# A Mamba-like mixer and a Hadamard FFN on one core: order of the prologue and of the FFN's residual work

## The chip, the cores and the metric

One core of a Trainium2 chip runs the whole kernel in one launch. The metric is the device time in microseconds (us), the median of three runs. Engines: PE (TensorE), DVE (VectorE), ACT (ScalarE), POOL (GpSimd), and SP (SyncE), which only issues DMAs here.

## The reference

The input `u` has 4 batches of 512 tokens by 256 channels. `c` (4 x 256) gives six vectors per batch, shift, scale and gate for each of two halves:

```
sa, ca, ga, sb, cb, gb = silu(c) @ wmod          (ga, gb: sign(g) * max(|g|, 0.25))
h = layernorm(u) * (1 + ca) + sa
xBC, z, A = split(h @ W_in.T)                    32 heads, head 8 wide, state 64
x, B, C = split(causal_conv4(xBC) + conv_b)
M[l, s] = (C_l . B_s) * exp(segsum(-softplus(A)))  for s <= l, per head
y = M x + D x ;  u1 = u + ga * (y * silu(z + z_bias)) @ W_out.T
h2 = layernorm(u1) * (1 + cb) + sb
out = u1 + gb * fwht(silu(h2 @ W1.T) * (h2 @ W3.T)) @ W2.T     hidden 1024
```

All of it is float32.

## The kernel before, in words

Every engine has one instruction stream, written out by hand, with semaphores between them; the order in the text is the order on the engine. A matrix product that needs float32 is made of three matmuls with high and low parts (`split_mm`, L334 to L336).

The **prologue** works by batch b of u. DVE makes the statistics (L938 to L944) and, with the inverse root from POOL (L1260), the normalised rows `xn` (L951). PE transposes them with the identity out of `cst` into banks 2 and 3 (L356). ACT applies shift and scale (`h32`, L700) and copies a high part (L704), POOL subtracts the low part (L1266). PE then projects: the decay inputs from `h32` (`a_project`, L387), two channel tiles of x from the high and low parts (`x_project`). ACT does the convolution's last tap of each tile with its bias (L711), DVE the other three (L974). The tiles of x go to DRAM by SP, and through PE transposes (L402) and an ACT copy (L718) into `x_tok`. The decays go through softplus (ACT L732 to L737, DVE L1009), a running sum (DVE L1013), DRAM, and back as rows broadcast over the partitions. In between PE makes the modulation vectors (`modulation`, L345) and the gate rows (L366), which go over DRAM into `gates`. While it waits for data PE does `warm` matmuls on zeros (L425).

The **loop** has 8 groups of 4 heads by 4 batches, 32 units. For each unit PE projects four tiles of B and C (`proj`), ACT and DVE do the taps (L751, L1054), PE makes scores (L499), ACT the decays (L789), DVE `mix` (L1042), PE the states (L518), the inter and intra parts (L534, L543). A unit's stages stand in three successive steps. POOL masks the sums rows (L1317) and splits weights. Before the loop proper the units of group 0 are written out: unit (0,0) with the prologue, then step(0,1), (0,2), (0,3).

The **tail** is the FFN by batch: `up` (8 hidden tiles m: two products of 512 columns, silu on ACT, `hid` L1183 and `hid_lo` L1190 on DVE) and `down` (L334 to L336 with 256 columns). The front of the next batch is put in between the hidden tiles: the sum of y at m = 0, the gate (L1082) at m = 2, the output projection (PE L603) at m = 4, two residuals of two instructions each (L1145, L1149) at m = 6, the statistics at m = 7.

Of the kernel before, what the change touches and what calls it, by code (L numbers as in the profile page):

```python
# [46 lines left out]
def adaln_ssm_ffn_kernel(nc, u, w_bc, w_x, w_a, w_z, conv, d_rows, z_bias, w_out, w13, w2, c_t, wmod,  # L47
                         consts, out, sums_d, gates_d):
    with ExitStack() as ctx:
# [279 lines left out]
        def _(pe):  # L329
# [40 lines left out]
            def x_project(b):  # L370

                pe.wait_ge(s["hlo_done"], KT * (b + 1))
                for xt in range(2):
                    if b >= 2:
                        pe.wait_ge(s[f"xtaps{xt}"], 3 * (b - 1))
                    for kt in range(KT):
                        i = split_mm(ps[:, GT * (b % 2) + xt, :], wx_hi[:, xt, kt, :], wx_lo[:, xt, kt, :],
                                     ht_hi[:, kt, b * L:(b + 1) * L], ht_lo[:, kt, b * L:(b + 1) * L],
                                     kt == 0, kt == KT - 1)
                    i.then_inc(s["xp_mm"], 1)  # L380
# [11 lines left out]
            def x_transposes(b):  # L392

                for xt in range(2):
                    n = 2 * b + xt
                    pe.wait_ge(s[f"xtaps{xt}"], 3 * (b + 1))
                    if n >= 2:
                        pe.wait_ge(s["xtok_ev"], n - 1)
                    else:
                        pe.wait_ge(s["h32_done"], KT * B)  # L400
                    for c in range(CH):
                        i = nc.tensor.transpose(ps[:, 2 + xt, c * P:(c + 1) * P],  # L402
                                                acc[:, n // GT, n % GT, c * P:(c + 1) * P], ident)
                    i.then_inc(s["xT_mm"], 1)
# [1076 lines left out]
```

## Time and profile before

| | |
|---|---|
| three timed runs | 585.65, 585.75, 586.25 us (median 585.75) |
| the profiled execution | 584.53 us, span 582.7 us, mean granted clock 0.994 |
| busy share of the span | PE 97%, DVE 81%, ACT 66%, POOL 35% |
| DMA | 70.93 MB, mean 122 GB/s |

How to read it: "start, us" are microseconds from the span's start; "idle before <-" is the engine's idle time ahead of an instruction and what ended it. PE's ends are modelled, since matmuls overlap, so its start times are the firmer numbers. PEclk is the clock that was granted to PE as a share of full speed.

### The profile page before, as it was taken

Reading aid. Unit: us, or ns where it says so; the run is one execution under the profiler, and the core shown is the slowest. Engines: PE = TensorE matmul, PEld = TensorE weight load, DVE = VectorE, ACT = ScalarE, POOL = GpSimd, SP = SyncE. Lnnn points to the kernel's source line nnn. Section 1 sums busy time; section 2 is a strip of 40 time slices with the busy share of each in tenths; the row PEclk is TensorE's granted clock in tenths of the full one; section 3 lists DMA queues with packets and bytes.
Section 4 is the critical chain, followed back from the end, with each engine's and each line's share of the span. In section 5 each row is a group of like instructions: output and inputs, shape, how many; then the busy total and the mean of one; then the engine's idle time right before and its main releaser. Section 6 shows DMA issues by size and latency. Waiting matters only on the chain.

```text
span 582.7 us, 18096 instructions
## 1 busy us (share of the span) xinstructions
PE 563.0 (97%) x6693; PEld 452.1 (78%) x6694; DVE 472.7 (81%) x753; ACT 386.8 (66%) x960; POOL 206.2 (35%) x377
## 2 busy tenths in 40 slices
PE   7899999999999999999999999999998998998997
PEld 3577677778778787777777877877687987988987
DVE  6789999989989989988999999999657637637443
ACT  2588788788888888877878888887633223332340
POOL 4742265464464365686245243445000000000000
PEclk9799999999999999999999999999999999999999
DMA  8535544533534535533443447456423034100101
GB/s 288 231 115 191 152 142 121 163 116 114 163 106 126 162 108 194 165 109 108 132 147 112 126 151 192 149 162 176 133 74 108 1 97 120 37 2 0 37 0 37
DMA packets 39516, 70.93 MB, mean 122 GB/s; under 512 B 4532, under 2 KB 10804, under 8 KB 39224
## 3 DMA queue, kind: packets, MB, share of 16 engines
q1 hardware_dynamic: 39480, 70.47, 38.6%
q8 instruction: 20, 0.33, 0.2%
q14 instruction: 16, 0.13, 0.1%
HBM read 57.34 MB, written 13.12 MB: 121 GB/s over the span
## 4 chain that ended last, share of the span: by engine, by line
PE 81%; DVE 9%; ACT 3%; issue 3%; DMA 2%; POOL 1%; SPq 0%; DVEq 0%; ACTq 0%; POOLq 0%
PE ps L334 17%; PE ps L336 16%; PE ps L335 16%; PE ps L499 10%; PE ps L543 5%; PE ps L482 4%; PE ps L534 4%; PE ps L518 4%; PE ps L603 2%; DVE acc L1054 2%; DMA u_sb<-in_u 1%; DVE mix L1042 1%; DVE hid_lo L1190 1%; PE ps L356 1%; PE ps L387 1%
## 5 line engine op out<-in xcount | busy, mean ns | idle before, releaser
L1054 DVE SCALAR_TENSOR_TENSOR acc<-ps,cw_dve,acc 128x511 f32<-128x511 f32 (+2 forms) x384 | 259.1, 739 | 2.9 <-ACT acc L751 1.4
L789 ACT ACTIVATE decay<-sums,p_slot 128x128 f32<-128x128 f32 x512 | 160.6, 396 | 1.3 <-DVE mix L1042 0.5
L1317 POOL TENSOR_SCALAR_AFFINE_SELECT sums<-sums 128x512 f32<-128x512 f32 x128 | 81.6, 640 | 180.6 <-DMA sums<-running_sums 172.7
L751 ACT ACTIVATE acc<-ps,cw_act 128x512 f32<-128x512 f32 x128 | 93.2, 776 | 48.9 <-PE ps L543 45.4
L334 PE MATMUL ps<-ht_hi,wg_hi 128*128 128x512 f32 x256 | 106.9, 418 | 2.0 <-POOL wg_lo L1255 1.1
L336 PE MATMUL ps<-ht_hi,wg_lo 128*128 128x512 f32 x256 | 101.1, 395 | 0.0
L335 PE MATMUL ps<-ht_lo,wg_hi 128*128 128x512 f32 x256 | 101.0, 395 | 0.0
L1042 DVE TENSOR_TENSOR mix<-ps,decay 128x1024 f32<-128x1024 f32 x64 | 78.0, 1219 | 20.6 <-PE ps L499 19.3
L499 PE MATMUL ps<-acc 64*64 64x64 f32 (+1 forms) x2048 | 69.8, 255 | 0.7 <-DVE mix L1042 0.7
L889 ACT ACTIVATE silu_sb<-ps 128x512 f32<-128x512 f32 x32 | 19.2, 599 | 77.3 <-PE ps L336 77.3
L499 PEld LDWEIGHTS ps<-acc 64*64 64x64 f32 x2048 | 54.4, 132 | 9.7 <-issue 9.0
L334 PEld LDWEIGHTS ps<-ht_hi,wg_hi 128*128 128x128 f32 x256 | 48.1, 188 | 14.7 <-issue 1.5
L1183 DVE TENSOR_TENSOR hid<-ps,silu_sb 128x512 f32<-128x512 f32 x32 | 22.1, 691 | 45.5 <-ACT silu_sb L889 45.5
L336 PEld LDWEIGHTS ps<-ht_hi,wg_lo 128*128 128x128 f32 x256 | 48.0, 187 | 11.7
L1260 POOL TENSOR_TENSOR rstd<-vareps,minus_half 128x4 f32<-128x4 f32 x8 | 8.2, 1027 | 135.4 <-DVE vareps L944 131.7
L335 PEld LDWEIGHTS ps<-ht_lo,wg_hi 128*128 128x128 f32 x256 | 48.2, 188 | 7.7
L334 PE MATMUL ps<-h_hi,w_hi 128*128 128x512 f32 x128 | 50.7, 396 | 0.8 <-DVE h_lo L1164 0.8
L336 PE MATMUL ps<-h_hi,w_lo 128*128 128x512 f32 x128 | 49.9, 390 | 0.0
L335 PE MATMUL ps<-h_lo,w_hi 128*128 128x512 f32 x128 | 49.9, 389 | 0.0
L334 PE MATMUL ps<-w_hi,hid_hi 128*128 128x256 f32 x128 | 36.9, 288 | 5.0 <-DVE hid_lo L1190 4.8
L335 PE MATMUL ps<-w_lo,hid_hi 128*128 128x256 f32 x128 | 36.2, 283 | 0.0
L336 PE MATMUL ps<-w_hi,hid_lo 128*128 128x256 f32 x128 | 36.2, 282 | 0.0
(136 smaller groups left out, 897.4 us busy)
## 6 DMA issues: line engine op xcount, KB each, us to landing
sums<-running_sums SPq DMA_DIRECT2D x128, 256.0 KB, 3.3
y_parts<-yt_sb SPq DMA_DIRECT2D x32, 256.0 KB, 2.0
wg_raw<-in_w_bc SPq DMA_DIRECT2D x8, 512.0 KB, 4.6
stage<-y_parts SPq DMA_DIRECT2D x16, 256.0 KB, 4.2
u_sb<-in_u SPq DMA_DIRECT2D x4, 512.0 KB, 7.1
stage<-in_w SPq DMA_DIRECT2D x1, 2048.0 KB, 15.3
x_channels<-acc SPq DMA_DIRECT2D x8, 256.0 KB, 2.3
ee<-decay_rows SPq DMA_DIRECT2D x8, 256.0 KB, 4.4
```

Source lines behind the costliest of these rows:

```text
L334: mm(o, w_hi, x_hi, start=first, stop=False)
L335: mm(o, w_hi, x_lo, start=False, stop=False)
L336: return mm(o, w_lo, x_hi, start=False, stop=last)
L482: i = nc.tensor.transpose(ps[:, 6, c * P:(c + 1) * P], acc[:, b % 2, p, c * P:(c + 1) * P], ident)
L499: i = mm(ps[NS * h:NS * (h + 1), 2 + a, c * P + NS * h:(c + 1) * P], acc[own, b % 2, p, c * P + NS * h:c * P + NS * (h + 1)], acc[own, b % ...
L518: i = mm(o, b_tok[:, p, c * P + NS * a:c * P + NS * (a + 1)], xds[:, b % 2, V0[c]:V0[c] + n, HD * j:HD * (j + 1)], start=(c == 0), stop=(c ...
L543: i = mm(ps[QD * j:QD * j + YW, 7, c * P:(c + 1) * P], xs[:, b % 2, c, j, :], mix[:, j, c * P:(c + 1) * P], start=False, stop=True, skip_g ...
L751: af(acc[:, b % 2, t, :], ps[:, PROJ_BANK[t], :], ACT.Identity, bias=cw_act[:, t, 1:2], scale=cw_act[:, t, 0:1]).then_inc(s[f"tap_a{t}"], 1)
L789: i = af(decay[:, j, c * P:(c + 1) * P], sums[:, j, c * P:(c + 1) * P], ACT.Exp, scale=-1.0, bias=p_slot[:, b * CH + c, j:j + 1])
L1042: tt(mix[:, 2 * p:2 * p + 2, :], ps[:, 2:4, :], decay[:, 2 * p:2 * p + 2, :], ALU.mult).then_inc(s["mixed"], 1)
L1054: stt(a[:, d:], ps[:, PROJ_BANK[t], 0:L - d], cw_dve[:, t, TAPS - 1 - d:TAPS - d], a[:, d:], ALU.mult, ALU.add).then_inc(s[f"taps{t}"], 1)
L1317: gp.affine_select(out=v, in_=v, compare_op=ALU.is_ge, fill=FAR, base=0, pattern=[[0, CH], [1, P]], channel_multiplier=-1).then_inc(s["mas ...
```

## The change

SP loads batch 1 of u right behind batch 0, then the identity alone; the other constants come behind `wz`. The norms of batches 0 and 1 are made together, and of 2 and 3; the transposes of batch 1 go to banks 4 and 5 (the warming matmuls to bank 1), so that they need not wait for ACT. `a_project(0)` stands ahead of `norm_transposes(2)`. The x projections, transposes and copies, the h, high and low parts are now issued by tile instead of by batch, and interleaved. `last_tap` of the first two units waits for its own tile's transpose, and for all x stores of its half. The first step of the loop, (0,1), is written out for PE and ACT with the last x tiles between its parts. The store of the gate rows and their broadcasts stand elsewhere on SP. In the tail the gate is at m = 1, the output projection at m = 3, the residuals at m = 4 and 5, the statistics at m = 6. A line "..." stands for unchanged or left out lines.

**SP**

```diff
- load(cst[:], consts, "ld_cst")
+ load(u_sb[:, CH:2 * CH, :], u_b[1], "ld_u1")
+ load(cst[:, 0:1, :], consts[:, 0:1, :], "ld_ident")
...
- load(u_sb[:, CH:2 * CH, :], u_b[1], "ld_u1")
...
+ load(cst[:, 1:, :], consts[:, 1:, :], "ld_cst")
...
+     elif b:
+         sp.wait_ge(s["gate_ev"], 1)
+         sp.dma_start(gates_d, xn[0:B, 0, 0:2, :].rearrange("b k d -> b (k d)")).then_inc(s["st_gates"], 16)
...
- sp.wait_ge(s["gate_ev"], 1)
- sp.dma_start(gates_d, xn[0:B, 0, 0:2, :].rearrange("b k d -> b (k d)")).then_inc(s["st_gates"], 16)
+ step(0, 2, 0)
...
- for b in range(2, B):
-     step(0, b, 0)
+ step(0, 3, 0)
...
```

**PE**

```diff
-     if b:
-         pe.wait_ge(s["h32_done"], KT * b)
+     if b >= 2:
+         pe.wait_ge(s["h32_done"], KT * (2 * b - 3))
...
-             i = nc.tensor.transpose(ps[:, 2 + kt, c * P:(c + 1) * P],
+             i = nc.tensor.transpose(ps[:, (4 if b == 1 else 2) + kt, c * P:(c + 1) * P],
...
-         mm(ps[:, 5, :], zeros[:, 0:P], zeros[:], start=True, stop=True)
+         mm(ps[:, 1, :], zeros[:, 0:P], zeros[:], start=True, stop=True)
...
- pe.wait_ge(s["ld_cst"], 16)
+ pe.wait_ge(s["ld_ident"], 16)
...
- warm(8)
...
- norm_transposes(2)
+ warm(10)
...
+ norm_transposes(2)
...
- x_project(0)
+ x_project(0, 0)
+ x_project(0, 1)
...
- x_project(1)
+ x_project(1, 0)
+ x_project(1, 1)
...
- x_project(2)
- x_transposes(0)
- x_project(3)
+ x_project(2, 0)
...
- x_transposes(1)
+ x_transposes(0, 0)
+ x_project(2, 1)
+ x_transposes(0, 1)
+ x_project(3, 0)
...
+ x_project(3, 1)
+ x_transposes(1, 0)
...
+ x_transposes(1, 1)
...
- x_transposes(2)
...
+ x_transposes(2, 0)
...
- x_transposes(3)
+ x_transposes(2, 1)
...
- for b in range(1, B):
-     step(0, b, gq=0, gr=(None if b == 1 else 0))
+ proj(0, 1, 1)
+ proj(0, 1, 0)
+ x_transposes(3, 0)
+ x_transposes(3, 1)
+ proj(0, 1, 3)
+ b_transposes(0, 0, 0, True)
+ proj(0, 1, 2)
+ scores(0, 0, 0, True)
+ b_transposes(0, 0, 1, True)
+ for b in range(2, B):
+     step(0, b, gq=0, gr=0)
...
-             if m == 4:
+             if m == 3:
...
```

**ACT (h_parts and x_evacuate are cut into h_full, h_high and x_evacuate of one tile; h of batch 1 reads banks 4 and 5)**

```diff
- h_parts(0)
- h_parts(1)
+ h_full(0, 0)
+ h_full(0, 1)
+ h_full(1, 0)
+ h_high(0, 0)
+ h_full(1, 1)
+ h_high(0, 1)
+ h_high(1, 0)
+ h_high(1, 1)
+ h_full(2, 0)
+ h_high(2, 0)
+ h_full(2, 1)
...
- h_parts(2)
...
+ h_high(2, 1)
...
- h_parts(3)
+ h_full(3, 0)
+ h_full(3, 1)
...
+ h_high(3, 0)
+ h_high(3, 1)
...
- x_evacuate(0)
+ x_evacuate(0, 0)
...
+ x_evacuate(0, 1)
+ x_tap(3, 1)
...
-     if not (isinstance(n, int) and n < 2):
+     if isinstance(n, int) and n < 2:
+         act.wait_ge(s["xT_mm"], GT * n + t + 1)
+         act.wait_ge(s[f"st_x{n}"], 16 * GT)
+     else:
...
- x_tap(3, 1)
- x_evacuate(1)
+ x_evacuate(1, 0)
...
- act.wait_ge(s["st_x0"], 16 * GT)
- act.wait_ge(s["xT_mm"], GT)
...
- x_evacuate(2)
+ x_evacuate(1, 1)
+ last_tap(0, 0, 3)
...
- last_tap(0, 0, 3)
...
- x_evacuate(3)
- act.wait_ge(s["xn_done"], CH * B)
- af(e_rows, sums_t[:], ACT.Exp, scale=-1.0).then_inc(s["e_rows"], 1)
...
+ act.wait_ge(s["p_copy"], 1)
+ head_rows(0)
+ decays(0, 0, 0, True)
+ gate_size()
+ x_evacuate(2, 0)
+ last_tap(0, 1, 1)
+ x_evacuate(2, 1)
+ last_tap(0, 1, 0)
+ act.wait_ge(s["xn_done"], CH * B)
+ af(e_rows, sums_t[:], ACT.Exp, scale=-1.0).then_inc(s["e_rows"], 1)
+ decays(0, 0, 1, True)
+ x_evacuate(3, 0)
...
- act.wait_ge(s["p_copy"], 1)
- for b in range(1, B):
-     step(0, b, gq=0, gr=(None if b == 1 else 0), first=(b == 1))
+ b_evacuate(0, 0)
+ x_evacuate(3, 1)
+ last_tap(0, 1, 3)
+ last_tap(0, 1, 2)
+ decays(0, 0, 2, True)
+ b_evacuate(0, 1)
+ decays(0, 0, 3, True)
+ for b in range(2, B):
+     step(0, b, gq=0, gr=0)
...
```

**DVE**

```diff
+ statistics1(1)
...
- statistics1(1)
+ normalise1(1)
...
- normalise1(1)
+ statistics1(3)
...
- statistics1(3)
...
- for b in range(2):
-     for k in range(TAPS - 1):
-         x_tap(b, 0, k)
-         x_tap(b, 1, k)
+ x_tap(0, 0, 0)
+ x_tap(0, 1, 0)
+ x_tap(0, 1, 1)
+ x_tap(0, 0, 1)
+ x_tap(0, 0, 2)
+ x_tap(1, 0, 0)
+ x_tap(0, 1, 2)
+ x_tap(1, 0, 1)
+ x_tap(1, 1, 0)
+ x_tap(1, 0, 2)
+ x_tap(1, 1, 1)
...
+ x_tap(1, 1, 2)
+ x_tap(2, 0, 1)
...
- x_tap(2, 1, 0)
+ modulation(1)
...
- x_tap(2, 0, 1)
+ x_tap(2, 1, 0)
...
+ x_tap(2, 0, 2)
...
- x_tap(2, 0, 2)
...
- modulation(1)
...
+ x_tap(3, 0, 1)
+ x_tap(3, 1, 1)
...
- x_tap(3, 0, 1)
- x_tap(3, 1, 1)
+ x_tap(3, 1, 2)
...
- x_tap(3, 1, 2)
...
- for t in (0, 2):
-     for k in range(TAPS - 1):
-         tap(0, 0, t + 1, k)
-         tap(0, 0, t, k)
+ tap(0, 0, 1, 0)
+ tap(0, 0, 0, 0)
+ tap(0, 0, 1, 1)
+ tap(0, 0, 0, 1)
+ tap(0, 0, 1, 2)
+ tap(0, 0, 3, 0)
+ tap(0, 0, 0, 2)
+ tap(0, 0, 2, 0)
+ tap(0, 0, 3, 1)
+ tap(0, 0, 2, 1)
+ tap(0, 0, 3, 2)
+ gate_rows()
+ tap(0, 0, 2, 2)
...
-             if m == 2:
+             if m == 1:
...
+             if m == 4:
+                 residual1(b + 1, 0)
+             if m == 5:
+                 residual1(b + 1, 1)
...
-                 residual1(b + 1, 0)
-                 residual1(b + 1, 1)
-             if m == 7:
...
```

**POOL (h_low takes one tile)**

```diff
+ inverse_root(1, "eps1", "rs")
...
- inverse_root(1, "eps1", "rs")
...
- h_low(0)
+ h_low(0, 0)
+ h_low(0, 1)
...
- h_low(1)
+ h_low(1, 0)
+ h_low(1, 1)
+ h_low(2, 0)
...
+ h_low(2, 1)
...
- h_low(2)
- h_low(3)
+ h_low(3, 0)
...
+ h_low(3, 1)
...
+     if n_first(n):
+         own_x(g, n, b, early)
+         mask(n, 2)
...
-     mask(n, 2)
-     own_x(g, n, b, early)
+     if not n_first(n):
+         mask(n, 2)
+         own_x(g, n, b, early)
...
```

## Rows read from the trace of the kernel before

**Rows 1.** busy us of each engine (instructions), granted clock, DMA share, GB/s, by stretch

```profile
5.00:10.00 5.00, 4.34 (x28) 2.75 (x27) 3.38 (x14) 0.00 (x0) 1.01 (x1) 1.00 0.98 327
100.00:150.00 50.00, 50.00 (x789) 39.63 (x789) 46.96 (x66) 41.91 (x115) 23.98 (x48) 1.00 0.44 133
```

**Rows 2.** PE's timeline, 70 to 90 us: start, us, what; the `states` blocks

```profile
75.06 0.87 PE L518 MATMUL ps<-xds,b_tok 128*64 128x24 f32 x24
...
86.12 0.87 PE L518 MATMUL ps<-xds,b_tok 128*64 128x24 f32 x24
```

**Rows 3.** chain of waits, first 80 us: start, us, what

```profile
2.90 6.79 DMA u_sb<-in_u
...
26.60 0.87 PE ps L356 x8
27.47 0.23 PE ps L334
```

**Rows 4.** PE's timeline, 0 to 40 us

```profile
8.29 1.95 PE L345 MATMUL ps<-c_silu,wmod_sb 128*128 128x4 f32 x16 [0.66 <-DMA wmod_sb<-in_wmod]
...
15.76 1.97 PE L356 MATMUL ps<-cst,xn 128*128 128x128 f32 x8 [2.86 <-DVE xn L951]
...
23.54 0.50 PE L334 MATMUL ps<-ht_hi,wx_hi 128*128 128x512 f32 x1
```

**Rows 5.** PE's waits, 425 to 583 us: total us, times, longest

```profile
PE ps L334 <- DVE hid_lo L1190: 4.8, 3, 1.7
```

**Rows 6.** DVE's timeline, 0 to 80 us

```profile
4.80 1.40 DVE L938 BATCH_NORM_STATS2 stats<-u_sb 128x6 f32<-128x256 f32 x4 [1.08 <-DMA u_sb<-in_u]
...
12.49 1.39 DVE L938 BATCH_NORM_STATS2 stats<-u_sb 128x6 f32<-128x256 f32 x4
...
14.32 1.38 DVE L951 TENSOR_SCALAR xn<-u_sb,meanvar,rstd 128x256 f32<-128x256 f32 x4
15.85 3.10 DVE L951 TENSOR_SCALAR xn<-u_sb,meanvar,rstd 128x256 f32<-128x256 f32 x4 [0.15 <-POOL rstd L1260]
...
27.04 8.62 DVE L974 SCALAR_TENSOR_TENSOR acc<-ps,conv_sb,acc 128x511 f32<-128x511 f32 x13 [1.61 <-ACT acc L711]
...
62.59 1.20 DVE L1042 TENSOR_TENSOR mix<-ps,decay 128x1024 f32<-128x1024 f32 x1
```

**Rows 7.** POOL's timeline, 0 to 80 us

```profile
15.57 2.57 POOL L1266 TENSOR_TENSOR ht_lo<-h,ht_hi 128x512 fp32r<-128x512 f32 x2
```

**Rows 8.** ACT's timeline, 0 to 80 us

```profile
12.61 1.45 ACT L700 ACTIVATE h<-ps,shift,scale 128x512 f32<-128x512 f32 x2 [10.03 <-DVE scale L982]
13.95 1.13 ACT L704 CAST ht_hi<-h 128x512 fp32r<-128x512 f32 x2
```

**Rows 9.** waits of PE (23.5 to 75 us), then of DVE (26 to 63 us)

```profile
PEld ps L334 <- DVE acc L1054: 1.1, 2, 0.6
...
PEld ps L410 <- DVE scale L982: 0.9, 1, 0.9
PEld ps L334 <- DVE acc L974: 0.9, 1, 0.9
...
PE ps L499 <- DVE mix L1042: 0.7, 1, 0.7
...
DVE acc L974 <- ACT acc L711: 2.6, 2, 1.6
DVE acc L1054 <- ACT acc L751: 1.2, 2, 0.7
DVE sp_a L1009 <- ACT a_work L737: 0.8, 1, 0.8
```

**Rows 10.** timelines of ACT and DVE, 468 to 505 us

```profile
489.09 0.60 ACT L889 ACTIVATE silu_sb<-ps 128x512 f32<-128x512 f32 x1 [1.61 <-PE ps L336]
...
491.33 0.69 DVE L1183 TENSOR_TENSOR hid<-ps,silu_sb 128x512 f32<-128x512 f32 x1
```

**Rows 11.** a window of 1 us, columns as in rows 1

```profile
16.00:17.00 1.00, 1.00 (x6) 1.00 (x6) 1.00 (x2) 0.00 (x0) 1.00 (x2) 0.50 0.83 265
```

More of the change, by code:

```diff
@@ L368, in gate_rows, with x_project @@
                 i.then_inc(s["gate_mm"], 1)
-            def x_project(b):
+            def x_project(b, xt):
                 pe.wait_ge(s["hlo_done"], KT * (b + 1))
[L373 to L380, printed above, removed]
+                if b >= 2:
+                    pe.wait_ge(s[f"xtaps{xt}"], 3 * (b - 1))
+                for kt in range(KT):
+                    i = split_mm(ps[:, GT * (b % 2) + xt, :], wx_hi[:, xt, kt, :], wx_lo[:, xt, kt, :],
+                                 ht_hi[:, kt, b * L:(b + 1) * L], ht_lo[:, kt, b * L:(b + 1) * L],
+                                 kt == 0, kt == KT - 1)
+                i.then_inc(s["xp_mm"], 1)
             def a_project(b0):
@@ L390, in a_project, with x_transposes @@
                             i.then_inc(s["a_mm"], 1)
[L392 to L404, printed above, removed]
+            def x_transposes(b, xt):
+                n = 2 * b + xt
+                pe.wait_ge(s[f"xtaps{xt}"], 3 * (b + 1))
+                if n >= 2:
+                    pe.wait_ge(s["xtok_ev"], n - 1)
+                else:
+                    pe.wait_ge(s["h32_done"], KT * B)
+                for c in range(CH):
+                    i = nc.tensor.transpose(ps[:, 2 + xt, c * P:(c + 1) * P],
+                                            acc[:, n // GT, n % GT, c * P:(c + 1) * P], ident)
+                i.then_inc(s["xT_mm"], 1)
             def p_transposes():
@@ L574, in step @@
                 q = gq * B + bq
-                r = gr * B + br if gr is not None else None
-                first = r is None
+                r = gr * B + br
                 proj(g, b, 1)
-                if r is not None:
-                    states(r, br)
-                    scores(r, br, 1, False)
-                b_transposes(q, bq, 0, first)
+                states(r, br)
+                scores(r, br, 1, False)
+                b_transposes(q, bq, 0, False)
                 proj(g, b, 0)
@@ L584, in step @@
                 proj(g, b, 2)
-                if r is not None:
-                    inter(r, br, isinstance(r, int) and r == 0)
-                    intra(r, br)
-                scores(q, bq, 0, first)
-                b_transposes(q, bq, 1, first)
+                inter(r, br, isinstance(r, int) and r == 0)
+                intra(r, br)
+                scores(q, bq, 0, False)
+                b_transposes(q, bq, 1, False)
             pe.wait_ge(s["st_zero"], 1)
             pe.wait_ge(s["xs_zero"], 1)
-            for b in range(1, B):
-                step(0, b, gq=0, gr=(None if b == 1 else 0))
+            proj(0, 1, 1)
[9 more added lines that the diff above has]
+                step(0, b, gq=0, gr=0)
             with pe.Fori(1, NG) as g:
@@ L662, in _ @@
             pe.wait_ge(s["bfly"], 6)
+            pe.wait_ge(s["ld_cst"], 16)
             w2_transform(0)
@@ L690, in _, with h_full, h_high @@
             af(c_exp[:], c_sb[:], ACT.Exp, scale=-1.0).then_inc(s["c_exp_done"], 1)
[L692 removed]
+            def h_full(b, kt):
+                n = KT * b + kt
                 act.wait_ge(s["lnT_mm"], b + 1)
[L695 to L704 removed]
+                if b >= 2:
+                    act.wait_ge(s["hlo_done"], n - 3)
+                    act.wait_ge(s["a_mm"], 2)
+                af(h32[:, b % 2, kt, :], ps[:, (4 if b == 1 else 2) + kt, :], ACT.Identity, bias=shift[:, 0, kt, b:b + 1],
+                   scale=scale1[:, 0, kt, b:b + 1]).then_inc(s["h32_done"], 1)
+            def h_high(b, kt):
+                act.wait_ge(s["h32_done"], KT * b + kt + 1)
+                nc.scalar.copy(ht_hi[:, kt, b * L:(b + 1) * L], h32[:, b % 2, kt, :]).then_inc(s["hhi_done"], 1)
             def x_tap(b, xt):
@@ L816, in gate_size, with step @@
                 af(xn[0:B, 0, 0:2, :].rearrange("b k d -> b (k d)"), ps[0:B, 7, :], ACT.Abs).then_inc(s["gate_abs"], 1)
-            def step(g, b, gq, gr, first=False):
+            def step(g, b, gq, gr):
                 bq = (b - 1) % B
                 q = gq * B + bq
-                r = gr * B + (b - 2) % B if gr is not None else None
+                r = gr * B + (b - 2) % B
                 if b == 0:
@@ L837, in step @@
                 last_tap(g, b, 0)
-                decays(q, bq, 2, first)
-                if first:
-                    gate_size()
+                decays(q, bq, 2, False)
                 b_evacuate(q, 0)
@@ L1097, in step @@
                 tap(g, b, 0, 2)
-                if first:
-                    gate_rows()
                 mix_pair(q, 0, first)
@@ L1306, in own_x @@
             def own_x(g, n, b, early):
+                if isinstance(n, int) and n < B:
+                    pool.wait_ge(s["xtok_ev"], 2 * (n + 1))
                 if not early:
@@ L1335, in y_add, with n_first @@
                 gp.tensor_tensor(yi[:, kt, :], yi[:, kt, :], yo[:, kt, :], ALU.add).then_inc(s["ysum"], 1)
+            def n_first(n):
+                return isinstance(n, int) and n == 0
             def step(g, b, split=False, ffn_tile=None, front=False):
```

57 lines of the change are left out of this document (22 added, 35 removed).

## The prediction

> **What bounds the kernel now.** I read, in this order, the windows of the whole run, the starts of one recurring block on PE, the chain of waits over the first 80 us, the timelines of PE, DVE, POOL and ACT there with their waits, and the same for the last 130 us. In the steady part PE is never idle: 50.00 of 50 us in the window from 100 to 150 [rows 1]. The `states` block (L518) comes every 11.06 us (86.12 - 75.06) [rows 2], one step's work of PE. So from 75.06 on the time is PE's own work, and what the prologue saves up to there the kernel keeps. The reader is to see two places where PE waits. In the prologue the chain runs over the second batch of u: its load is issued at 2.90 and lands 6.79 us later, at 9.69 [rows 3], and PE's first x projection starts only at 23.54, after spells like the 2.86 us before the norm transposes at 15.76 [rows 4]. In the tail PE stands three times, 4.8 us in all, before a part of the down projection, for `hid_lo` from DVE [rows 5].
>
> **Base.** The rows are of an execution of 584.53 us (span 582.7, with 1.8 around it, which nothing here touches). The median of the three runs is 585.75, 1.22 above; I take the saving off both.
>
> **Prologue.** Batch 0 of u is issued as before, its statistics begin as before, at 4.80 [rows 6]. Ahead of batch 1 now stands neither the 320 KB of constants nor the 512 KB of modulation columns. From 5 to 10 us the loads ran at 327 GB/s [rows 1]: 832 KB are 2.6 us, so it lands at about 7.1. The modulation columns have 256 KB more ahead of them (batch 1 and 64 KB of identity for 320 KB), 0.8 us: PE's modulation (1.95 us) starts at 9.1 instead of 8.29 [rows 4] and ends at 11.0.
>
> DVE: a batch's statistics take 1.9 us (12.49 to 14.41), an undisturbed normalisation 1.38; the two from 14.32 and 15.85 show what disturbs one [rows 6]: beside POOL's two `ht_lo` (15.57 to 18.14) [rows 7] four instructions took 3.10 us. So DVE's plain normalisation waits out POOL's. Statistics 0 and 1 then run from 4.8 to 9.0, normalisation 0 to 10.4, normalisation 1 to 11.8; POOL's split of wx now falls on it (its second half is an instruction of the size of an `ht_lo`, 2.57 us for two, [rows 7]), so I put it at 13.0 and the copies of the modulation at 13.1. Bounds: 11.8 with no disturbance, 13.7 with 1.9 us of it, and the start of the x projections moves with it. The Trainium skill (SBUF — State Buffer, section "SBUF: two separate sides") states a rule that speaks against this reordering: POOL and DVE's two-port instructions hold one port pair as an exclusive lock, the second comer blocked for the whole of the other's instruction. The trace agrees: 3.10 for 1.38 us. By the strict rule both instructions of the split can hold normalisation 1, which would make the time 0.7 us more than my sum; by mere sharing of bandwidth it would be up to 1.2 less.
>
> ACT takes 0.73 for an h and 0.57 for a high part [rows 8]. From 13.1 it does h(0,0), h(0,1), h(1,0), high(0,0), h(1,1): 16.5. Before, batch 1's transposes themselves began only at 15.76 [rows 4], since DVE had statistics 2 ahead and the banks were batch 0's. PE: transposes of batches 0 and 1 (0.87 each, [rows 3]) end at 13.9, ten warming matmuls of 0.23 reach 16.2, the decay projection (8 x 0.23 = 1.84) 18.3. POOL's low parts of batch 0 (2.57 for two) [rows 7] begin behind the first high part at 15.9 and end at 18.5. DVE: statistics 2 and 3 to 17.0, normalisation 2 waits for the low parts as at 15.85 and ends at 19.1, PE transposes it to 20.0. x_project(0,0) starts at 20.0 instead of 23.54: **3.5 us**.
>
> From here on DVE is the bound. Its first x tap came at 27.04, behind four ACT instructions on batch 2; now behind three (0.73 + 0.57 + 0.73): 20.0 + 0.1, then to 22.1, x tap of 0.7, so DVE starts at 22.8, 4.2 us earlier. The taps (8.62 for 13, [rows 6]) are all still there. Up to the first `mix` at 62.59 DVE waited for ACT 1.0 + 1.2 + 0.8 = 3.0 us (2.6 less the 1.61 of the 27.04 row) [rows 6, 9]; the new order hands it tiles one by one and the x taps of batch 3 come ahead of the exponentials, so by the same durations none of these stay. I see one new wait, 0.7 us at its second tap, where ACT does a high part between the x taps. First `mix`: 62.59 - 4.2 - 3.0 + 0.7 = 56.1, 6.5 earlier. PE can follow: between 23.54 and 75.06 its weight loads waited 0.9 + 0.9 + 1.1 us for DVE [rows 9], and 0.7 before the scores for the `mix`; 3.5 + 3.6 = 7.1 is the most that it can gain. Against the 6.5 stands one new wait: the first unit's scores need the last x evacuation, which ACT now does behind a decay and a b evacuation; 0.5 us of it I take to show. **Prologue 6.0 us.** Bounds: 2.0 (the 3.5 of the start, nothing of the waits, 1.5 lost again) and 7.3 (normalisation 1 undisturbed).
>
> Moved and hidden: the other constants come behind wz, no one needs them before the tail. The store of the gate rows goes ahead of the last sums row of step 1, the broadcasts behind step 2, so SP no longer holds step 2's sums rows through the round trip; it was hidden by PE's work, and counts nothing. The x stores are waited for at the first taps, and land well before, since xtaps are earlier too. POOL is busy 24 of 50 us in the loop [rows 1], and one mask changes place. The two transposes, b and x, cost PE the same wherever they stand.
>
> **Tail.** In each of the first three FFN batches DVE puts four residual instructions of the size of `hid` (0.69) and the statistics (1.9) between hidden tiles 5 and 7. For tile 7 silu was ready at 489.09 + 0.60, but `hid` started at 491.33 [rows 10], 1.6 us late, and PE's seventh part behind it. PE needs 12 x 0.23 = 2.7 us per tile, DVE 1.3, so 1.4 is free per tile. Now the first two residual instructions (1.4) take the gap before tile 4, the next two that before tile 5, the statistics that before tile 6 (0.5 late), and tile 7 is on time. The gate's products go before tile 1, where DVE has nothing to do: the z projection is ahead of up(1) on PE. The output projection costs the same at tile 3. The last batch, which has none of this, adds no such wait to the three [rows 5]. So the 4.8 us go: **4.8**, at the least 3.5 (a rest of 0.4 each), at the most 5.1 with the drained pipeline's restarts.
>
> Sum: 6.0 + 4.8 = 10.8. 584.53 - 10.8 = 573.7 for a profiled execution, 585.75 - 10.8 = 575.0 for the median.
>
> **Rivals.**
> (a) *The clock falls on the x projections.* PE had idled from 12.9; the granted clock was 0.50 (the 1.2 GHz level) from 16 on, although PE was busy all that microsecond with transposes [rows 11]; by 27.47 the pitch is 0.23 again [rows 3]. In the new order PE only waits and transposes from 18.3 to 20.0. If the level is the lower one after that, 12 matmuls cost 0.23 more each, on the path: 2.5 us with the transposes slower too. Time 575.0 + 2.5 = 577.5. Against: warming matmuls and decay projection come just before, and 1.7 us are less than 2.86. Chance 0.22.
> (b) *The saving is eaten before the loop*: batch 1 lands late, or ACT's in-order queue starves DVE at other places than before. Of the prologue 3.0 reaches `states`: 585.75 - 3.0 - 4.8 = 578.0. For it: ACT is idle little from here on and works strictly in order, on waits for three engines. Chance 0.15.
> (c) *The tail keeps its stalls*: a residual now waits for its load or the statistics still end late. 585.75 - 6.0 - 0.5 = 579.3. Chance 0.04.
> (d) *Slower.* The clock stays at the lower level from the early transposes far into the projections. A microsecond there costs 0.5 us of PE's work, so from 22 us on all 10.8 are gone; at 26 us the time is 588.0. In the trace the low spell ends before 27.47, under 12 us. Chance 0.03, and 0.02 for a shorter one that leaves no change.
> (e) *More*: normalisation 1 undisturbed, and PE free of waits from 19.2: 7.3 + 5.1, 573.4. Chance 0.10.
> The forecast has 0.44.
>
> **Numbers.** 0.2% is about what a measurement of this kernel can tell from no change. Faster 0.95, same 0.02, slower 0.03. The range 572.8 to 578.5 holds the forecast, (a), (b) and (e).
>
> **What would show it.** Statistics of batch 1 right behind those of batch 0, near 7; x projection at 20; first x tap on DVE near 22.8; first `mix` near 56; the second L518 block near 69 instead of 75.06, and the next 11.06 later; granted clock 1.00 between 16 and 24 (else a); in the tail `hid` of tile 7 within 0.1 us of its silu and no wait for `hid_lo`. The prediction is wrong if PE idles more between 25 and 65 us than it did, or if the period of `states` grows.

## The result, and the profile after

| | before | changed |
|---|---|---|
| median (lowest to highest), us | 585.70 (585.10 to 586.25) | 575.23 (574.59 to 575.64) |
| ratio, 95% interval | | 0.9820 (0.9803 to 0.9837) |
| profiled execution / span | 584.53 / 582.7 | 575.64 / 573.9 |
| busy PE, DVE, ACT, POOL | 97, 81, 66, 35% | 98, 82, 67, 36% |

The median fell by 10.5 us where 10.8 were forecast (575.0). The profiled pair differs by 8.9 only: that execution of before was 1.2 us under its median and that of the changed kernel 0.4 over it. So the parts below are read from that pair and checked with the experiments' medians. Two more executions of the changed kernel, in its repeated run, took 782 and 1097 us in another, slow state; they are left out of every number below.

PE's steady part is what it was. Its timeline, 55 to 90 us, answers to [rows 2]: start, us, what.

```profile
60.10 0.87 PE L524 MATMUL ps<-xds,b_tok 128*64 128x24 f32 x24
71.17 0.87 PE L524 MATMUL ps<-xds,b_tok 128*64 128x24 f32 x24
82.22 0.87 PE L524 MATMUL ps<-xds,b_tok 128*64 128x24 f32 x24
```

The block that stood at 75.06 is at 71.17, 3.9 us earlier, and the period is 11.05 still. What is saved in front of it is kept. PE's prologue, 0 to 26 us, against [rows 4]:

```profile
1.21 6.41 PE L425 MATMUL ps<-sums 128*128 128x512 bf16 x20 [1.21 <-DVE sums L968]
10.01 1.95 PE L347 MATMUL ps<-c_silu,wmod_sb 128*128 128x4 f32 x16 [2.39 <-DMA wmod_sb<-in_wmod]
11.82 3.54 PE L358 MATMUL ps<-cst,xn 128*128 128x128 f32 x16
15.48 2.11 PE L425 MATMUL ps<-sums 128*128 128x512 bf16 x9
17.52 1.91 PE L388 MATMUL ps<-h,wa_sb 128*32 128x512 f32 x8
19.36 1.09 PE L358 MATMUL ps<-cst,xn 128*128 128x128 f32 x8
20.21 0.48 PE L336 MATMUL ps<-ht_hi,wx_hi 128*128 128x512 f32 x1
...
24.86 1.09 PE L358 MATMUL ps<-cst,xn 128*128 128x128 f32 x8 [1.60 <-DVE xn L993]
```

The first x projection starts at 20.21 (forecast 20.0). But PE then waits 1.60 us for DVE, which was not forecast. DVE's timeline, 4 to 34 us, against [rows 6]:

```profile
4.74 1.41 DVE L980 BATCH_NORM_STATS2 stats<-u_sb 128x6 f32<-128x256 f32 x4 [1.47 <-DMA u_sb<-in_u]
...
6.59 1.40 DVE L980 BATCH_NORM_STATS2 stats<-u_sb 128x6 f32<-128x256 f32 x4
...
8.43 3.13 DVE L993 TENSOR_SCALAR xn<-u_sb,meanvar,rstd 128x256 f32<-128x256 f32 x8
...
15.90 2.35 DVE L993 TENSOR_SCALAR xn<-u_sb,meanvar,rstd 128x256 f32<-128x256 f32 x4
20.49 4.31 DVE L993 TENSOR_SCALAR xn<-u_sb,meanvar,rstd 128x256 f32<-128x256 f32 x4 [2.24 <-PE ps L358]
24.73 7.56 DVE L1016 SCALAR_TENSOR_TENSOR acc<-ps,conv_sb,acc 128x511 f32<-128x511 f32 x11
```

Statistics of batch 1 follow those of batch 0 without a gap, so batch 1 of u had landed. Normalisation 3 starts at 20.49 and takes 4.31 us for four instructions that take 1.38 undisturbed, so the first x tap comes at 24.73, not at 22.8. POOL's timeline, 4 to 26 us, shows both reasons (against [rows 7]):

```profile
14.27 1.01 POOL L1318 TENSOR_TENSOR rstd<-vareps,minus_half 128x4 f32<-128x4 f32 x1 [1.51 <-DVE vareps L986]
16.75 2.65 POOL L1323 TENSOR_TENSOR ht_lo<-h,ht_hi 128x512 fp32r<-128x512 f32 x2 [1.48 <-ACT ht_hi L718]
19.36 1.01 POOL L1318 TENSOR_TENSOR rstd<-vareps,minus_half 128x4 f32<-128x4 f32 x1
20.35 3.90 POOL L1323 TENSOR_TENSOR ht_lo<-h,ht_hi 128x512 fp32r<-128x512 f32 x3
```

The inverse root of batch 3 stands behind two low parts and ends at 20.37; the next low parts then run beside the normalisation that it released. DVE's row names PE as its releaser. But the wait for PE in front of normalisation 3 (L1005 of the changed kernel) is for the transposes of batch 1, which ended before 15.5; the root ends 0.12 us before normalisation 3 starts, and in the repeated run below POOL is named.

The windows of the prologue: us, busy us of PE, PEld, DVE, ACT, POOL, granted clock, DMA share, GB/s.

```profile
11.00:12.00 1.00, 1.00 (x11) 1.00 (x11) 0.56 (x2) 0.00 (x0) 0.92 (x2) 0.98 1.10 402
12.00:13.00 1.00, 1.00 (x6) 1.00 (x5) 1.00 (x5) 0.00 (x0) 0.75 (x1) 0.50 1.05 411
...
15.00:16.00 1.00, 0.88 (x5) 0.52 (x5) 0.96 (x8) 0.81 (x2) 0.27 (x1) 0.81 0.56 156
16.00:24.00 8.00, 7.25 (x36) 3.89 (x34) 5.76 (x7) 6.38 (x12) 7.25 (x6) 1.00 0.82 332
```

The clock falls to the 1.2 GHz level at 12, four microseconds earlier than before [rows 11], after 2.39 us without work and a spell of the narrow modulation matmuls; from 16 it is full, also while PE makes the x projections. All 16 transposes of batches 0 and 1 (11.82, 3.54 us) fall into the low spell; what that cost is read below, in the run with more warming.

In the tail PE's waits, 416 to 574 us, hold no `hid_lo` any more (4.8 us, [rows 5]), and nothing took its place: total us, times, longest.

```profile
PE ps L336 <- DVE h_lo L1221: 0.8, 1, 0.8
PE ps L336 <- DVE stage L1257: 0.2, 1, 0.2
```

The last hidden tiles of a batch, ACT's silu and DVE's `hid` of tile 7, against [rows 10]:

```profile
483.40 0.60 ACT L931 ACTIVATE silu_sb<-ps 128x512 f32<-128x512 f32 x1 [1.61 <-PE ps L338]
```

```profile
479.80 1.40 DVE L980 BATCH_NORM_STATS2 stats<-x_tok 128x6 f32<-128x256 f32 x4
...
481.64 0.69 DVE L1241 TENSOR_TENSOR hid<-ps,silu_sb 128x512 f32<-128x512 f32 x1
...
484.03 0.69 DVE L1241 TENSOR_TENSOR hid<-ps,silu_sb 128x512 f32<-128x512 f32 x1 [1.09 <-ACT silu_sb L931]
```

Silu of tile 7 ends at 484.00 and `hid` starts at 484.03, where it was 1.6 us late. The statistics make tile 6 0.4 late (480.68 + 0.60 to 481.64), which PE doesn't see.

### The profile page after: what moved, and what is told of

It reads as the page before. It is cut to its first block, busy times and chain, and to the rows that moved or that the text cites. A ratio compares the mean times of both kernels' runs of the same rounds, so it can differ in the third digit from the quotient of the medians.

```text
span 573.9 us, 18109 instructions
## 1 busy us (share of the span) xinstructions
PE 561.3 (98%) x6695; PEld 452.1 (79%) x6696; DVE 472.6 (82%) x753; ACT 387.3 (67%) x960; POOL 207.6 (36%) x377
## 4 chain that ended last, share of the span: by engine, by line
PE 88%; DVE 6%; DMA 2%; issue 1%; POOL 1%; ACT 1%; SPq 0%; DVEq 0%; ACTq 0%; POOLq 0%
PE ps L336 18%; PE ps L338 18%; PE ps L337 18%; PE ps L505 11%; PE ps L549 5%; PE ps L488 5%; PE ps L540 4%; PE ps L524 4%; PE ps L615 2%; DVE acc L1104 2%; DVE acc L1016 1%; DMA wmod_sb<-in_wmod 1%; PE ps L358 1%; PE ps L561 1%; PE ps L388 1%
```

## The experiments

"Changed" stands for the changed kernel. Medians in us. The kernel before had 585.59, 585.69, 585.53 and 584.76 in the four groups of runs: the repeated run, the two parts and the early root; the warming between, alone and with the early root, the banks and the loads; more warming, POOL held and the first with the low parts on DVE; the last run. The changed kernel ran with the result (575.23) and in the first group (574.99) only. So for the other groups the ratio to the kernel before is the fairer measure; its interval is 0.8 to 1.7 us either way.

The kernel before has two kinds of executions: 21 of its 38 had a mean granted clock of 0.993 or 0.994 and a median of 584.9, the other 17 had 0.991 or less and 586.1. Its profiled one is of the first kind (0.994), and so are all four of the tail alone. No trace of the second kind was kept, so where they lose their time is open. In the last group only two of nine were of it, which goes with that group's lower median.

**The changed kernel again**, no edit.

> The changed kernel again, for the size of the saving. Theory: the prologue saves 3.9 us (states of unit 1 at 71.17 instead of 75.06) and the tail 4.9, 8.8 together, and the 10.5 between the medians is in part the spread of executions: the ratio comes out between 0.982 and 0.985. Rival: the profiled pair is not typical and the saving is 10.5 or more, ratio 0.982 or less in five rounds.

574.99; ratio 0.9820 (0.9805 to 0.9834), on the edge between the theory and its rival, so it decides between neither; profiled 574.72, span 572.9. PE's and DVE's rows that differ:

```profile
8.16 1.95 PE L347 MATMUL ps<-c_silu,wmod_sb 128*128 128x4 f32 x16 [0.18 <-DMA wmod_sb<-in_wmod]
...
14.14 3.30 PE L425 MATMUL ps<-sums 128*128 128x512 bf16 x10
```

```profile
19.55 4.11 DVE L993 TENSOR_SCALAR xn<-u_sb,meanvar,rstd 128x256 f32<-128x256 f32 x4 [0.15 <-POOL rstd L1318]
23.58 0.74 DVE L1016 SCALAR_TENSOR_TENSOR acc<-ps,conv_sb,acc 128x511 f32<-128x511 f32 x1
```

The same program: the modulation columns landed at 8.16 instead of 10.01. Behind it h, POOL's low parts (15.75 for 16.75), the third root and the first tap are 1.0 to 1.2 us earlier, and the span is 1.0 shorter. How a late landing brings the late tap is seen in the run with more warming.

**One part alone.** First the changed kernel with the old tail:

```diff
-                         if m == 3:
+                         if m == 4:
...
-                         if m == 1:
+                         if m == 2:
...
-                         if m == 4:
+                         if m == 6:
                              residual1(b + 1, 0)
-                         if m == 5:
                              residual1(b + 1, 1)
-                         if m == 6:
+                         if m == 7:
```

> The changed kernel with the tail of before (gate at m=2, output projection at 4, residuals at 6, statistics at 7). Theory (the two parts add up): the three waits for hid_lo of 4.8 us come back, the saving over the kernel before is that of the prologue alone, 3.9 to 5.5 us, ratio 0.991 to 0.993. Rival (the tail's place costs or gains something else, as clock or DMA): the saving differs from 4 to 5.5 by more than 1 us.

Then the kernel before with these same lines the other way round, the new tail alone:

> The kernel before with only the new tail. Theory: 4.9 us less than before, ratio 0.9915; no wait of PE for hid_lo in the FFN. Rival: the old prologue shifts nothing here, so if it gains less than 4 us the stalls were partly hidden by something else.

Old tail: 580.20, 0.9909 (0.9895 to 0.9924), so the prologue alone saves 5.4. Tail alone: 580.06, 0.9906 (0.9892 to 0.9921), so it saves 5.5. Together 10.9, against 10.6 measured for both in the same group of runs: the two add up within their intervals. The traces price the tail in another way, by the span less the start of the first x tap: 578.4 - 24.30 = 554.1 with the old tail against 549.2 for the changed kernel, and 582.7 - 27.04 = 555.66 before against 578.0 - 27.36 = 550.64 with the tail alone. That is 4.9 and 5.0 us. Part of the 5.5 of the medians is thus the clock of the kernel before: against its five executions at 0.993 or 0.994 in that group (median 584.90) the tail alone saves 4.8 and the prologue alone 4.7. PE's waits in the tail of the one with the old tail:

```profile
PE ps L336 <- DVE hid_lo L1247: 4.8, 3, 1.7
```

**The third root ahead of the low parts.**

```diff
              inverse_root(2, "eps1", "rs")
+             inverse_root(3, "eps1", "rs")
              h_low(0, 0)
              h_low(0, 1)
-             inverse_root(3, "eps1", "rs")
```

> The changed kernel with one line moved on POOL: the inverse root of batch 3 ahead of the low parts of batch 0. Theory (the third missing piece of the prologue is normalisation 3, which waits for its root until 20.4 and then stands beside three low parts, 4.31 us, and holds PE's transposes to 24.86 and DVE's first x tap to 24.73): normalisation 3 ends by 21.5, first x tap near 23.3, PE's wait of 1.6 us gone, kernel 1.2 to 1.6 us faster than the changed one. Rival (DVE's taps or ACT set the pace anyway): under 0.4 us; or the low parts of batch 0 come 1 us later and it is slower.

574.48, 0.9809 (0.9796 to 0.9821): 0.5 under the changed kernel in the same group, less than half of what was expected, and within the noise. DVE's rows, and POOL's:

```profile
17.85 5.06 DVE L993 TENSOR_SCALAR xn<-u_sb,meanvar,rstd 128x256 f32<-128x256 f32 x4 [0.15 <-POOL rstd L1318]
24.09 0.75 DVE L1016 SCALAR_TENSOR_TENSOR acc<-ps,conv_sb,acc 128x511 f32<-128x511 f32 x1 [1.19 <-ACT acc L725]
```

```profile
17.57 6.50 POOL L1323 TENSOR_TENSOR ht_lo<-h,ht_hi 128x512 fp32r<-128x512 f32 x5
```

Normalisation 3 starts early and then stands beside four of five low parts in a row (5.06). It ends 0.7 us sooner than in the repeated run, but the tap waits for ACT and comes 0.5 us later than there (24.09 for 23.58). In this execution the clock was at 0.50 from 11 to 17, PE's ten warming matmuls took 3.96 us for 3.30, and without a pause behind them the x projection started only at 20.91 (for 20.30).

**Warming matmuls between the transposes**, alone and with the early root.

```diff
              norm_transposes(0)
+             warm(5)
              norm_transposes(1)
```

> The changed kernel with five more warming matmuls between the transposes of batch 0 and of batch 1, where PE idles or transposes and after which the granted clock fell to 0.50 in each of the four new-order traces. Theory (the low clock costs PE time ahead of the decay projection only, and the x projections wait for normalisation 2 on DVE): the clock stays at 1.00 or its low spell is shorter, the decay projection starts at 16.4 to 16.6 instead of 17.4, but x_project(0,0) stays at 20.0 to 20.3; 0 to 0.4 us faster than the changed kernel. Rival (the clock is what the prologue lost): 1 us or more faster.

575.04, and a wide interval, 0.9828 (0.9800 to 0.9857): three executions at 574.4, 575.0 and 574.4, two at 578.2 and 578.4. The profiled one is of the latter; its PE rows and two windows:

```profile
13.93 2.34 PE L425 MATMUL ps<-sums 128*128 128x512 bf16 x5
16.06 1.91 PE L358 MATMUL ps<-cst,xn 128*128 128x128 f32 x8
```

```profile
12.00:14.00 2.00, 2.00 (x11) 1.94 (x12) 2.00 (x7) 0.00 (x0) 0.62 (x1) 0.50 1.05 413
...
16.00:18.00 2.00, 1.98 (x9) 1.79 (x9) 1.97 (x11) 0.00 (x0) 0.28 (x1) 0.50 0.49 171
```

Columns late (9.95), clock at 0.50 from 12 to 18: five warming matmuls cost 2.1 us in front of the second transposes (13.93 to 16.06), and the first tap comes at 27.23. So rival (a)'s mechanism exists, at another place: these matmuls were on the path while the clock was low. ACT's third h waits for the second transposes (18.01), and POOL's low parts start at 19.37 for 16.75. The tap is 2.5 us later than in the changed kernel's own execution with late columns (24.73).

> Both edits: root of batch 3 ahead of the low parts of batch 0, and the five warming matmuls. Theory: the root's move alone put x_project(0,0) at 20.9 since the low parts came 1.8 us later and PE's warm matmuls ran at the low clock; with the clock up it is DVE's normalisations beside POOL's low parts that are left: 0.5 to 1.0 us faster than the changed kernel, about 574.4. Rival (two edits that each pay add up, if the clock had held the first back): 573.5 or less.

With both edits: 574.47, 0.9814 (0.9797 to 0.9830), near the theory's 574.4 by the median and 0.4 under the changed kernel by ratio, which is within the noise. The clock is 1.00 throughout in the profiled execution; the x projection there waits 1.2 us for `ht_lo`, until 20.22, and the first tap comes at 22.84, when normalisation 3 ends.

**The banks: batch 1 transposed into banks 2 and 3 again.**

```diff
-                 if b >= 2:
-                     pe.wait_ge(s["h32_done"], KT * (2 * b - 3))
+                 if b:
+                     pe.wait_ge(s["h32_done"], KT * b)
...
-                         i = nc.tensor.transpose(ps[:, (4 if b == 1 else 2) + kt, c * P:(c + 1) * P],
+                         i = nc.tensor.transpose(ps[:, 2 + kt, c * P:(c + 1) * P],
```

> The changed kernel with the transposes of batch 1 in banks 2 and 3 as before, waiting for the two h of batch 0. Theory (own banks are worth what ACT's two h take, but part of it is hidden, since x_project(0,0) waits for normalisation 2): h of batch 1 starts near 16 instead of 14.4, decay projection 1.5 us later, x projection 0.5 to 1.0 us later, kernel 0.5 to 1.0 slower than the changed one. Rival (banks are on the path in full): 1.5 to 2 us slower.

577.68, 0.9871 (0.9851 to 0.9890): the own banks are worth 2.5 us by the medians and 3.0 by ratio, more than either side said, though the intervals leave room for the rival's 2. PE:

```profile
14.84 1.94 PE L358 MATMUL ps<-cst,xn 128*128 128x128 f32 x8 [2.89 <-ACT h L712]
17.00 3.54 PE L425 MATMUL ps<-sums 128*128 128x512 bf16 x9 [0.22 <-issue]
```

The wait of 2.89 was expected in kind. The low clock was not: it is at 0.50 from 14, still 0.56 in the microsecond after 19, and nine warming matmuls take 3.54 and the transposes 1.94. So the price of the banks holds a share of the clock, which no run separates.

**The order of the loads: modulation columns ahead of batch 1 of u.**

```diff
- load(u_sb[:, CH:2 * CH, :], u_b[1], "ld_u1")
...
+ load(u_sb[:, CH:2 * CH, :], u_b[1], "ld_u1")
```

> The changed kernel with the modulation columns loaded ahead of batch 1 of u (the identity ahead of both). Theory (two batches first is what the prologue's gain rests on): statistics 1 begin at 8.9 instead of 6.6, everything on DVE up to normalisation 2 is 1.5 to 2 us later, the kernel 1.5 to 2 us slower than the changed one. Rival (modulation's late landing cost as much as batch 1's early landing gave, since its landing was 8.1 in two traces and 10.0 in two): within 0.5 us of the changed kernel.

577.63, 0.9865 (0.9847 to 0.9883): two batches first are worth 2.5 us (2.6 by ratio), a little more than the 1.5 to 2 expected. Here too the clock is low, at 0.50 from 13 to 18, and its share is not separated. The modulation then starts at 7.52, and DVE's second statistics at 9.10:

```profile
9.10 1.41 DVE L980 BATCH_NORM_STATS2 stats<-u_sb 128x6 f32<-128x256 f32 x4 [2.06 <-DMA u_sb<-in_u]
```

**More warming ahead of the modulation** (`warm(20)` to `warm(30)`).

> The changed kernel with 30 warming matmuls ahead of the modulation instead of 20, so that PE has no idle spell whether the modulation columns land at 8.1 or at 10.0. Theory (the low clock of the early transposes comes with PE's idle spell before or between them, and costs little beyond normalisation 2's own time): the clock stays at 1.00 or falls later and shorter, executions lie closer together, median 0 to 0.6 us under the changed kernel's 575.3. Rival: the clock falls as before, no difference; or the ten more matmuls hold the modulation up, 1 us slower.

575.13, 0.9821 (0.9808 to 0.9835), clock 1.00 throughout in all five executions, and no gain. Against the repeated run the decay projection is 1.3 us earlier (16.11 for 17.37), but the x projection where it was (20.19 for 20.30), since its transposes wait 1.32 us for normalisation 2, and so is the tap (23.47 for 23.58): the low clock of that execution, from 13 to 16, had cost nothing. In the changed kernel's first execution it had. PE and ACT with more warming:

```profile
9.78 1.84 PE L347 MATMUL ps<-c_silu,wmod_sb 128*128 128x4 f32 x16
11.49 2.14 PE L358 MATMUL ps<-cst,xn 128*128 128x128 f32 x16
```

```profile
12.66 2.12 ACT L712 ACTIVATE h<-ps,shift,scale 128x512 f32<-128x512 f32 x3 [10.09 <-DVE scale L1024]
```

And ACT in that first execution:

```profile
13.75 1.45 ACT L712 ACTIVATE h<-ps,shift,scale 128x512 f32<-128x512 f32 x2 [11.12 <-PE ps L358]
```

The modulation starts almost as late here (9.78 for 10.01), but the transposes take 2.14 us for 3.54, the first h starts 1.1 us earlier, and the low parts, the third root and the tap follow (15.63 for 16.75, 18.12 for 19.36, 23.47 for 24.73). So of the 1.3 us between the two taps some 1.0 is the low clock on the transposes: late columns cost through the gap that they leave in front of the modulation. That is one execution; the medians of the two kernels do not differ.

**POOL held back.** With `warm(30)`:

```diff
              inverse_root(3, "eps1", "rs")
+             pool.wait_ge(s["xn_done"], CH * B)
              h_low(1, 0)
...
+             h_low(3, 1)
              split_tile(0, 3)
              split_tile(0, 2)
-             h_low(3, 1)
```

> As e9_warm30, and POOL holds the low parts of batch 1 back until normalisation 3 is done (and makes the last low part ahead of the splits of two weight tiles). Theory (normalisation 3 took 4.1 to 4.3 us for an undisturbed 1.38 because POOL's low parts ran beside it, port against port): it takes 1.4 us here and ends near 21; DVE's first x tap moves little, since ACT's x tap is ready only at 23.4; the kernel is 0.2 to 0.8 us faster than e9_warm30. Rival (the 4.1 us is something else, such as the memory or the semaphores): normalisation 3 still takes 3 us or more.

574.16, 0.9806 (0.9792 to 0.9819), 1.0 under more warming alone, where 0.2 to 0.8 was expected; the two intervals overlap. DVE:

```profile
17.32 2.43 DVE L993 TENSOR_SCALAR xn<-u_sb,meanvar,rstd 128x256 f32<-128x256 f32 x4
19.90 1.39 DVE L993 TENSOR_SCALAR xn<-u_sb,meanvar,rstd 128x256 f32<-128x256 f32 x4 [0.15 <-POOL rstd L1318]
23.83 0.75 DVE L1016 SCALAR_TENSOR_TENSOR acc<-ps,conv_sb,acc 128x511 f32<-128x511 f32 x1 [2.54 <-ACT acc L725]
```

Normalisation 3 takes 1.39 with POOL idle and 4.11 with POOL's low parts beside it: the conflict is shown. The tap is then ACT's, and in the profiled execution it is no earlier (23.83 for 23.47), so the start of the tap does not explain the lower median.

**DVE makes batch 0's low parts** between normalisations 2 and 3, both roots ahead, with `warm(30)` and the early `h_low(3, 1)`; first without the wait for `xn_done`, then with it.

```diff
+             for kt in range(KT):
+                 dve.wait_ge(s["hhi_done"], kt + 1)
+                 tt(ht_lo[:, kt, 0:L], h32[:, 0, kt, :], ht_hi[:, kt, 0:L].bitcast(F32),
+                    ALU.subtract).then_inc(s["hlo_done"], 1)
...
-             h_low(0, 0)
-             h_low(0, 1)
              inverse_root(3, "eps1", "rs")
+             pool.wait_ge(s["hlo_done"], KT)
+             pool.wait_ge(s["xn_done"], CH * B)
              h_low(1, 0)
```

> As e10_hold_low, but the low parts of batch 0 are made by DVE between normalisations 2 and 3 (0.69 each by the size) instead of by POOL beside normalisation 2 (1.28 each). Theory: normalisation 2 takes 1.4 instead of 2.4 us, x_project(0,0) starts at 19.2 to 19.5 instead of 20.3, DVE's first x tap at 21.7 to 22.3 instead of 23.6, the kernel 1.0 to 2.0 us faster than the changed one, 573.3 to 574.3. Rival (DVE is the bound of the prologue, so 1.4 us more work on it undo the start): within 0.5 us of e9_warm30.

> The low parts of batch 0 on DVE, as in the kernel before this one, and with them POOL's low parts of batch 1 held until normalisation 3 is done. A pattern in the runs so far: span less the start of DVE's first x tap was 548.8 to 549.3 us in ten kernels (572.1 - 23.05, 572.8 - 23.83, 572.6 - 23.47, 575.1 - 26.33, 572.9 - 24.09 among them). Theory that DVE's first x tap sets the whole kernel: normalisation 3 falls from 4.32 to about 1.4 us and ends near 20.2 instead of 23.1; the first tap is then set by ACT, whose x tap was issued at 21.29 in the kernel before this one, so it comes at 22.1; the span is 22.1 + 549.05 = 571.2, the profiled time 573.0 and the median 573.0 to 573.9. Rival 1, that the hold costs as much as it gives (POOL's low parts of batch 1 end near 23 and DVE waits at its sixth tap for the x projection of batch 1, some 0.5 to 1.0 us): the first tap is at 22.1 but the span 571.8 to 572.3, median 574.1 to 574.9. Rival 2, that the chip's base of the median is what moves and no order of the prologue does better: 574.9 or more.

Without the hold 574.92, 0.9817 (0.9803 to 0.9830), slower than its 573.3 to 574.3. With it 573.79 (573.49 to 574.22), 0.9804 (0.9782 to 0.9826), inside its 573.0 to 573.9, the best of all; its five executions all lie below those of the changed kernel (574.46 at the lowest). But the kernel before was 0.8 faster in that group of runs too (more of its executions had the higher clock), and the ratios' intervals overlap: by ratio it gains 0.9 us on the changed kernel, probable rather than certain. DVE:

```profile
17.94 1.29 DVE L1045 TENSOR_TENSOR ht_lo<-h,ht_hi 128x512 fp32r<-128x512 f32 x2
19.14 1.38 DVE L993 TENSOR_SCALAR xn<-u_sb,meanvar,rstd 128x256 f32<-128x256 f32 x4
22.33 0.75 DVE L1016 SCALAR_TENSOR_TENSOR acc<-ps,conv_sb,acc 128x511 f32<-128x511 f32 x1 [1.81 <-ACT acc L725]
```

**All that have the new tail, side by side**, from the profiled executions:

| kernel | first x tap | first `mix` | span | span less tap |
|---|---|---|---|---|
| changed | 24.73 | 58.44 | 573.9 | 549.2 |
| changed again | 23.58 | 57.29 | 572.9 | 549.3 |
| early root | 24.09 | 57.67 | 572.9 | 548.8 |
| warm between | 27.23 | 61.34 | 576.4 | 549.2 |
| warm between, early root | 22.84 | 56.67 | 572.1 | 549.3 |
| shared banks | 26.33 | 59.66 | 575.1 | 548.8 |
| columns first | 26.20 | 60.24 | 575.5 | 549.3 |
| more warming | 23.47 | 57.17 | 572.6 | 549.1 |
| POOL held | 23.83 | 57.16 | 572.8 | 549.0 |
| DVE low | 23.05 | 56.99 | 572.1 | 549.1 |
| DVE low, POOL held | 22.33 | 56.40 | 571.7 | 549.4 |

The taps differ by 4.9 us and the last column by 0.6. From its first x tap to the first `mix` DVE waits 0.8 us in all in the changed kernel, and PE follows. Within a traced execution an edit of this prologue is worth what it does to the start of that one instruction. The medians follow it less closely: more warming has a tap at 23.47 and 575.13, POOL held one at 23.83 and 574.16. The trace is one execution in four or five, and executions of one kernel differ by up to 1.2 us at a granted clock of 1.000 (the first with the low parts on DVE: 573.89 to 575.08).

## Why the prediction was right, and where not

*What bounds the kernel: right.* The period stayed, and what came before 75.06 and in the tail was kept. Between 25 and 65 us PE was busy for 39.35 us, before for 37.93, so it idles less, as it had to.

*Tail, 4.8: right.* The three waits went, tile 7 is on time, tile 6 is 0.4 late (0.5 said). From the first `mix` to the end the pair gives 520.1 - 515.5 = 4.6, from which the 0.3 below is already taken: 4.9; by medians 5.5, with an interval of some 0.9 either way; 4.9 and 5.0 by the traces of the experiments.

*Prologue, 6.0: the mechanism right, the size too large* (3.9 in the profiled pair, 75.06 - 70.03 = 5.0 against the repeated execution, 5.4 by medians, 4.7 against the executions of the kernel before with the higher clock). By its steps:
- Batch 1 of u by 7.1: right, its statistics start at 6.59. The early load and the own banks both carry the prologue's gain: some 2.5 us each when taken back one at a time.
- Modulation at 9.1: 10.01 and 8.16 in two executions. The forecast is their middle; that the landing varies by 1.9 us from one execution to the next was not in it, nor that a late one brings the low clock onto the transposes, some 1.0 us.
- Normalisation 1 by 13.0: the eight instructions end at 11.56 and 12.46, the first 0.2 us before the lower bound of 11.8. It gained nothing by it, since PE was still in its transposes until 15.4.
- Start of the x projections, 20.0: 20.21 and 20.30. Right in sum, though normalisation 2 did not have to wait as the forecast had it: it ended at 18.25 in the first execution, and PE came to its transposes at 19.36 straight from the decay projection.
- The first x tap at 22.8: 24.73 and 23.58. **This is the step that failed.** It counted ACT's instructions in front of the tap and not DVE's own: normalisation 3 is also in front of it. Normalisation 2 was made to wait for the low parts; that POOL's root of batch 3 is queued behind the same low parts, and that the next low parts block DVE once more, 2.7 to 2.9 us, was left out. The prediction followed ACT's queue up to the tap, and neither DVE's nor POOL's. With POOL held and the low parts on DVE the tap is at 22.33.
- From the tap to the first `mix`, 2.3 gained: 35.55 before, 33.71 after, 1.8. DVE's waits for ACT there fell from 3.0 behind the first tap to 0.8, so the forecast of 0.7 for the one new wait was close, though the wait comes at the twelfth tap and not at the second (in the repeated run 0.3 at the second and 0.4 later). From `mix` on, 0.5 lost again: 0.3.

So 2.31 + 1.84 - 0.26 = 3.9, against 4.2 + 2.3 - 0.5; 1.9 of the missing 2.1 is the tap, and some 1.0 of that the clock. That the median came out within 0.3 us all the same is in part luck. The prologue was forecast too large, and against that stands something that was not in the sum: before's profiled execution, from which all rows were read, was 1.2 below its median, and the changed one's was 0.4 above. Of the executions of before in the experiments 17 of 38 ran at the lower mean clock, which fits; it is not shown for the runs of the result, whose clocks are not on record.

*Rival (a)*: no x projection ran at the lower clock. The clock fell at 12 instead, on the transposes. Where PE then waited for DVE anyway it cost nothing (the repeated run); in the changed kernel's own profiled execution it cost some 1.0 us, and it fell on the path in the warming between and with the shared banks too. The price that the prediction gave (a), 12 matmuls at 0.23 more with slower transposes, adds up to at least 2.8 us and not 2.5; nothing else hangs on it. *(b)* is in part what happened: something between the start at 20 and the loop was eaten, on DVE by POOL rather than by ACT's order, and 1.0 to 2.1 us were lost, not 3.0. *(c), (d), (e)* did not occur; half of (e)'s condition did, normalisation 1 nearly undisturbed (3.13 us for eight instructions), without its gain.

The rule of the Trainium skill that the prediction weighed (SBUF — State Buffer, section "SBUF: two separate sides": a POOL instruction, or one of DVE in a two-port mode, holds the shared port pair to its end, and the other engine's waits) is borne out on DVE's side: 1.39 us with POOL idle, 4.11 to 5.06 with it. On POOL's side it is not seen: three low parts took 3.90 us beside normalisation 3 and 3.83 without it (POOL held). The rule was weighed for normalisation 1, where the disturbance was 0.4 and 1.2 us in the two executions, and not asked again for normalisation 3, where it was 2.7 to 2.9.

Open is what moves the landing of the modulation columns between 8.1 and 10.0 us, with the loads in one order; nothing was tried on it. Open is also what the own banks and the early load are worth at full clock: neither was taken back together with more warming.

## What to carry to other kernels

When a prologue is reordered, find the first instruction after which one engine hardly waits again, and follow every engine's queue up to it, that engine's own and the ones which release it; in the traces here the rest of the kernel moved with that start, one for one within 0.6 us. A short instruction that others hang on (here a root of 128x4) belongs ahead of bulk work on its engine, but pays in full only if the bulk work does not then run beside what it released. Giving a step its own PSUM banks can be worth as much as an earlier load: some 2.5 us each here. Before a median is compared with a forecast from one trace, see whether that trace is typical: here the one of the kernel before was 1.2 us faster than its median.

## What the runs showed of the hardware

- Two low parts took 1.29 us on DVE and 2.54 on POOL. POOL's are hardly slowed by DVE (1.30 each beside it, 1.28 alone), while DVE's four normalisation instructions (1.38 us together) take 3.1 to 3.3 us beside two low parts, 4.1 to 4.3 beside three and 5.06 beside four.
- A wait of 2.9 us on PE in front of transposes was followed by the 1.2 GHz level until nearly 20 (shared banks), and one of 2.4 to 2.7 in front of the modulation by 0.50 from 12 to 15 or to 18. A gap in front of the modulation is not needed: the repeated run had 0.18 us there and 1.46 in front of the second transposes, and 0.50 from 13 to 16. With more warming and no gap until those transposes were done the level stayed at 2.4 GHz.
- The same 16 transposes took 3.54 us with the clock at 0.50 for nearly all of them and 2.14 at 1.00.
- One load of the same program, behind the same others, landed at 8.16 in one execution and at 10.01 in another, 1.85 us apart.
